# Projection, scores, output and routing of a gated layer in one step list, with two pairs of the shared expert moved behind the expert loop

## The chip, the cores and the metric

The program runs on one NeuronCore of a Trainium2 chip. TensorE (PE), VectorE (DVE), ScalarE (ACT), GpSimd (POOL) and SyncE (SP, which only issues transfers here) each work through their own list of instructions in order and wait on semaphores. The metric is the device time of one execution in microseconds; the kernel before has a median of 432.96 us over three runs (429.26 to 433.13).

## The reference

x is 32 x 64 tokens of 256 numbers, ctx the same; all float32. Four sublayers follow each other (layernorm before each):

```
# 1 gated retention, weights shared by q, k, v
Q,K,V = xh@Wh, kh@Wh, vh@Wh                       # two heads of 128; k = v = ctx
A  = max(|sum over batch of (Q K^T / sqrt(128)) * D|, 1)   # one 64x64 matrix per head
Y  = groupnorm(A V) ;  x += tanh(g) * ((relu(x@wg) * Y) @ wo)
# 2 mixture of 32 experts, 4 per token, at most 128 tokens each, and a shared expert
scores = sigmoid(x@gate.T); best 4 groups of 8, best 4 experts in them; slot = running count
routed = sum over 4 of w * (relu2(x_e @ up[e].T) @ down[e].T)
shared = relu2(x @ shup.T) @ shdn.T ;  x += tanh(g) * (routed + shared)
# 3 masked softmax(x ctx^T / 16) ctx ;  4 ternary-weight gated MLP (256 -> 1024 -> 256), int8 activations
```

A sums over all 32 sequences, so no output of sublayer 1 can start before every score is made. The slot of a token is its place in the order of all tokens, so no token can be gathered before the last one is routed.

## The kernel before, in words

The 2048 tokens are 16 tiles of 128, worked on in 8 pairs (NP = 8). Each engine has a block of code, and in it `run_steps(eng, n, stages)` writes out steps 0, 1, 2, ...: in step t each stage (lag, function) of the list is issued for pair t - lag, in the order of the list. So lags and places in the lists set the order on each engine, and `hold` puts the waits. Stages: c.sync waits for DVE's own instruction before.

Stage one, the scores loop: DVE p1_stats and p1_norm (POOL takes the power -1/2 in between, L469 and L471), PE p1_t transposes, ACT copies, PE p1_p multiplies by the gram matrix, DVE copies (p1_pt), PE p1_s adds to the scores, and p1_v makes the values from a ring of two ctxT buffers that ACT loads. DVE then turns the scores into A (L1052 to L1065).

Stage two, output and routing. PE per pair: p2_o (output product, psum<-big,bda), p2_zt (transposes, L798), p2_w (gate product, psum<-big,wg), p2_y (psum<-wo,tr), p2_xt (transposes, L816), p2_lg (logits, psum<-gateT,xnT), p2_pos (positions, five small products), p2_su and p2_sd (shared expert up and down, psum<-xnT,shup and psum<-shdn,rh), p2_ix (slots, psum<-gram,ck). DVE makes the statistics (o_stats, x1), the gate (wy), the routing in 17 parts (route_a) and 4 (route_b), adds the shared expert (`shared`, L1091) and the slots (add_slots). ACT normalises, copies and squares; POOL makes the rstd and the routing weights.

```
run_steps(pe, NP, [
    (1, p2_w), (3, p2_sd), (2, p2_xt), (0, p2_o), (2, p2_lg), (3, p2_pos), (2, p2_su), (1, p2_y),
    (3, p2_ix), (0, p2_zt)])
```

Stage three, experts: 16 steps of two experts. ACT writes the token indices, POOL gathers the tokens (L513), PE multiplies, DVE copies, SP stores; DVE also makes the ternary weights beside it. POOL writes the mask rows before it (L499, L502). Stage four: POOL gathers the expert rows (L531), DVE combines them (L1247), and attention and the MLP follow in one list of stages; DVE enters it when the norm weights (c_lnw) are in.

SP's transfers in order: constants, x in pairs, 11 weights and tables (c_w2, after half of the values), the expert weights upT and dnT, ctx and ctxT whole (after all values), xn stores, the three MLP matrices, expert output stores, the norm weights.

## Time and profile before

| | |
|---|---|
| median of three runs | 432.96 us (429.26 to 433.13) |
| profiled execution | 435.07 us, span of its instructions 432.6 us |
| busy in the span | PE 305.3 (71%), DVE 301.9 (70%), ACT 212.5 (49%), POOL 185.9 (43%) |
| mean granted clock of PE | 0.862 |
| moved | 43.89 MB, mean 101 GB/s |

The chain that ended last is 37% PE, 27% DVE, 12% issue, 11% DMA and 8% POOL. Busy shares are means over four stages with different limits, so the rows below are cut by stage: scores loop to 46.3 us, output and routing to 184.2 us, experts to 243 us, combine, attention and MLP to the end. A row of the windows view has, behind the stretch and its length, the busy time and the number of instructions of each engine, the granted clock of PE, the busy share of the DMA engines and GB/s.

### The profile page before, as it was taken

To read this page: it belongs to the slowest core of one execution; us is meant where nothing else is said; L and a number is where in the kernel's file an instruction comes from. 1 tells how busy PE (TensorE), PEld (TensorE's weight loads), DVE (VectorE), ACT (ScalarE), POOL (GpSimd) and SP (SyncE) were. 2 spreads that over 40 slices of the span, in tenths; PEclk is the share of its full clock that TensorE was granted. 3 is DMA by queue.
4 is the path that set the end of the run, shared out by engine and by line. 5 is a ranking of instruction groups with operands and counts; after the bars stand their busy time and mean duration, and the time that the engine had idled before them with its cause. 6 is when DMAs were issued, how large, how long until landed. Compare 5 with 4: busy or idle time off the path is not lost.

```text
span 432.6 us, 6083 instructions
## 1 busy us (share of the span) xinstructions
PE 305.3 (71%) x1780; PEld 231.1 (53%) x1780; DVE 301.9 (70%) x940; ACT 212.5 (49%) x384; POOL 185.9 (43%) x310
## 2 busy tenths in 40 slices
PE   2998489999999997348879403558664776667755
PEld 1886367888888776236768202325333344344423
DVE  2463335779787887717668334677999999989981
ACT  1232135334433535313333001557678989799883
POOL 3220121322233211576554177777878777332010
PEclk9998889999999998859899855555869899889898
DMA  5444799300000160035575532222121221100011
GB/s 179 121 139 145 291 436 371 116 27 6 19 25 26 33 284 24 1 79 145 129 160 171 153 103 79 80 73 74 50 74 55 68 85 36 51 26 0 26 46 52
DMA packets 23056, 43.89 MB, mean 101 GB/s; under 512 B 3630, under 2 KB 18416, under 8 KB 22128
## 3 DMA queue, kind: packets, MB, share of 16 engines
q1 hardware_dynamic: 16176, 28.82, 18.7%
q0 software_dynamic: 4672, 12.59, 11.3%
q10 hardware_dynamic: 2176, 2.10, 1.5%
q8 instruction: 14, 0.23, 0.2%
q14 instruction: 18, 0.15, 0.1%
HBM read 35.11 MB, written 8.39 MB: 101 GB/s over the span
## 4 chain that ended last, share of the span: by engine, by line
PE 37%; DVE 27%; issue 12%; DMA 11%; POOL 8%; ACT 5%; SPq 0%; POOLq 0%; DVEq 0%; ACTq 0%
PE psum L726 32%; DMA xn<-xn_dram,tix 6%; POOL big L531 5%; DVE x_all L1247 4%; DVE ham L1314 3%; DVE dnT L1312 3%; DVE upT L1304 2%; ACT rh L558 2%; DMA rh<-in_ctxT_dram 2%; DMA big<-ye_dram,dst_all 1%; DVE x_all L1272 1%; DVE bnx L1018 1%; PE psum L877 1%; DVE bn L1250 1%; DVE x_all L1336 1%
## 5 line engine op out<-in xcount | busy, mean ns | idle before, releaser
L531 POOL DMA_INDIRECT big<-ye_dram,dst_all x64 | 67.5, 1055 | 32.9 <-issue 18.9
L726 PE MATMUL psum<-q_w,rh 128*128 128x512 bf16 x128 | 40.9, 454 | 15.0 <-DVE upT L1304 9.1
L1247 DVE SCALAR_TENSOR_TENSOR x_all<-big,wk_all,x_all 128x256 f32<-128x256 f32 x64 | 31.1, 485 | 19.4 <-DMA big<-ye_dram,dst_all 17.6
L513 POOL DMA_INDIRECT xn<-xn_dram,tix x32 | 32.9, 1028 | 21.4 <-ACT tix L635 9.8
L726 PE MATMUL psum<-shdn,rh 128*128 128x256 f32 x128 | 31.4, 401 | 4.5 <-ACT rh L558 3.5
L917 PE MATMUL psum<-ident,xn 128*128 128x128 f32 x32 | 6.6, 341 | 34.2 <-ACT xn L592 34.2
L726 PEld LDWEIGHTS psum<-shdn,rh 128*128 128x128 f32 x128 | 24.8, 199 | 10.5 <-ACT rh L558 7.0
L726 PE MATMUL psum<-xnT,shup 128*128 128x256 f32 x128 | 29.6, 384 | 0.0
L726 PEld LDWEIGHTS psum<-q_w,rh 128*128 128x128 bf16 x128 | 12.5, 111 | 31.6 <-issue 20.5
L558 ACT ACTIVATE xnT<-psum 128x512 f32<-128x512 f32 x32 | 19.0, 595 | 18.6 <-PE psum L816 9.7
L457 POOL TENSOR_SCALAR vex<-mvx 128x2 f32<-128x2 f32 x16 | 3.6, 226 | 55.6 <-DVE mvx L1021 55.1
L457 POOL TENSOR_SCALAR ve<-mv 128x2 f32<-128x2 f32 x16 | 7.0, 438 | 46.2 <-DVE mv L1021 36.0
L726 PEld LDWEIGHTS psum<-xnT,shup 128*128 128x128 f32 x128 | 23.7, 190 | 2.9
L917 PEld LDWEIGHTS psum<-ident,xn 128*128 128x128 f32 x32 | 4.2, 169 | 37.3 <-issue 22.5
L558 ACT ACTIVATE big<-psum 128x512 f32<-128x512 f32 x16 | 9.6, 597 | 28.6 <-PE psum L752 20.9
L877 PE MATMUL psum<-ident,xn 128*128 128x128 f32 x64 | 14.3, 313 | 13.0 <-DMA xn<-xn_dram,tix 12.8
L558 ACT ACTIVATE dnT<-psum,q_down 128x512 bf16<-128x512 f32 x32 | 21.8, 682 | 3.4 <-PE psum L726 3.4
L592 ACT ACTIVATE xn<-x_all,sh,rs 128x256 f32<-128x256 f32 x16 | 8.7, 594 | 28.4 <-POOL sh L462 28.4
L690 ACT ACTIVATE upT<-upT 128x1024 f32<-128x1024 f32 x16 | 16.9, 1058 | 10.8 <-DVE upT L1304 10.8
L592 ACT ACTIVATE zr<-psum,sh,rs 128x256 f32<-128x256 f32 x16 | 8.2, 560 | 28.5 <-POOL sh L462 28.5
L635 ACT ACTIVATE tix<-idxf 128x1 int32<-128x1 f32 x32 | 6.1, 198 | 32.2 <-PE psum L877 25.5
L1304 DVE SCALAR_TENSOR_TENSOR upT<-psum,cgu,upT 128x1024 f32<-128x1024 f32 x16 | 20.5, 1278 | 1.7 <-PE psum L726 1.7
(191 smaller groups left out, 892.5 us busy)
## 6 DMA issues: line engine op xcount, KB each, us to landing
upT<-in_upT_dram SPq DMA_DIRECT2D x1, 4096.0 KB, 12.1
dnT<-in_dnT_dram SPq DMA_DIRECT2D x1, 4096.0 KB, 21.5
ye_dram<-rh SPq DMA_DIRECT2D x16, 256.0 KB, 2.7
rh<-in_ctxT_dram ACTq DMA_DIRECT2D x8, 256.0 KB, 3.1
x_all<-in_x_dram SPq DMA_DIRECT2D x8, 256.0 KB, 2.8
ctx_all<-in_ctx_dram SPq DMA_DIRECT2D x1, 2048.0 KB, 28.3
ctxT_all<-in_ctxT_dram SPq DMA_DIRECT2D x1, 2048.0 KB, 32.8
xn_dram<-xn SPq DMA_DIRECT2D x8, 256.0 KB, 2.1
```

The source lines that it names most:

```text
L513: pl.indirect_dma_start(out=xe[:, s, e, :], out_offset=None, in_=xn_dram[:, :], in_offset=bass.IndirectOffsetOnAxis(ap=tix[:, s, e:e + 1], ...
L531: pl.indirect_dma_start(out=gath[:, s, t * TOPK + k, :], out_offset=None, in_=ye_dram[:, :], in_offset=bass.IndirectOffsetOnAxis(ap=dst_al ...
L558: return act.activation(dst_ap, src, func, **kw).then_inc(done, 1)
L592: act.activation(dest[:, s, t, :], src(t), ACT.Identity, scale=rsb[:, s, t:t + 1], bias=sh[:, s, t:t + 1]).then_inc(done, 1)
L690: act.activation(sqj, hh[:, s, t, :], ACT.Square, accum_out=sst[:, s, t:t + 1]).then_inc(ssd[t], 1)
L726: return pe.matmul(o, l, r, start=first, stop=last, skip_group_check=True)
L877: ins = pe.transpose(bank(2, K, 2 * P)[:, k, e * P:(e + 1) * P], xe[:, s, e, k * P:(k + 1) * P], ident[:, :])
L917: ins = pe.transpose(bank(4, K, 2 * P)[:, k, t * P:(t + 1) * P], xn[:, s, t, k * P:(k + 1) * P], ident[:, :])
L1247: c(dve.scalar_tensor_tensor(xt(i, t), gath[:, s, t * TOPK + k, :], w, xt(i, t), ALU.mult, ALU.add))
L1304: dve.scalar_tensor_tensor(hh[:, s, t, :].rearrange("p (b n) -> p b n", b=2), psum[:, 2:4, :], cgu[:, s, 1, t:t + 1], sg[:, t, :].rearrang ...
L1312: dve.tensor_tensor(hw[:, s, t, :], hh[:, s, t, :], lnw[:, :], ALU.mult).then_inc(hwd[t], 1)
L1314: dve.tensor_reduce(ham[:, s, t:t + 1], hw[:, s, t, :], AX.X, ALU.max, apply_absolute_value=True)\
```

## The change

The two stages become one list of steps per engine. PE's list holds the scores loop (lags 0, 1, 2), the values (lag 8, so behind the scores), the transposes of A (10) and the output and routing pieces (12 to 20). The shared expert is cut into quarters (up and down, two halves each) at lags 17 to 20, and is run for the first six pairs only (NSH = 6); pairs 6 and 7 follow behind the expert loop, added by DVE in steps 1 and 2 of the combine loop. ctxT is loaded once by ACT, in eight transfers at the start, and kept; ctx comes in two parts, since its space holds the transposed xn of all pairs (xnT8) until the shared expert has used it. DVE's token rows (te) go to ACT (token_rows), POOL's mask work too. Logits move to the bank of positions, slots and values.

```diff
-            run_steps(pe, NP, [(0, p1_t), (1, p1_v), (1, p1_s), (0, p1_p)])
...
             run_steps(pe, NP, [
-                (1, p2_w), (3, p2_sd), (2, p2_xt), (0, p2_o), (2, p2_lg), (3, p2_pos), (2, p2_su), (1, p2_y),
-                (3, p2_ix), (0, p2_zt)])
+                (15, p2_lg), (20, early(p2_sd(0))), (13, p2_w), (17, p2_ix), (13, p2_zt), (12, p2_o), (0, p1_t),
+                (8, p1_v), (18, early(p2_su(1))), (16, p2_pos), (10, p1_at), (17, early(p2_su(0))), (1, p1_p),
+                (14, p2_xt), (19, early(p2_sd(1))), (2, p1_s), (13, p2_y)])
...
+            pe.wait_ge(xeT3, NG)
+            pe.wait_ge(hr3, NG)
+            for n in range(NSH, NP):
+                for h in range(2):
+                    p2_su(h)(Item(n), n % 2)
+            for n in range(NSH, NP):
+                for tt in (1, 0):
+                    p2_sd(tt)(Item(n), n % 2)
```

The waits that matter for the shared bank, and SP's list:

```diff
             def p2_lg(i, s):
-                hold(pe, (xnT2, i.at(1, 1)), *free(lt2, i))
+                hold(pe, (xnT2, i.at(1, 1)), (vc1, min(i.c + 7, NP)), (rb, RB * (i.c - 2) + 1))
...
             def p2_pos(i, s):
-                hold(pe, (ra, i.at(RA, RA_MASK)), *free(rb, i, RB), *free(ia2, i))
+                hold(pe, (ra, i.at(RA, RA_MASK)), (rb, RB * (i.c - 1) + 4), (lt2, min(i.c + 2, NP)), (ia2, i.c))
...
+            load_x(Item(0))
+            sp.dma_start(ident[:, :], a["c_ident"]).then_inc(c_in, 16)
+            sp.dma_start(whT[:, :, :], a["whT"]).then_inc(c_in, 16)
+            load_x(Item(1))
...
+            sp.wait_ge(lg2, NP)
+            for h in range(2):
+                sp.wait_ge(su2[h], NSH)
+            sp.dma_start(ctx_all[:, 0:2 * NSH, :], cv[:, 0:2 * NSH, :]).then_inc(c_ctx, 16)
...
+            for h in range(2):
+                sp.wait_ge(su2[h], NP)
+            sp.dma_start(ctx_all[:, 2 * NSH:NT, :], cv[:, 2 * NSH:NT, :]).then_inc(c_ctx2, 16)
             sp.wait_ge(yc3, NG)
             sp.dma_start(lnw, a["lnw"].to_broadcast([P, I])).then_inc(c_lnw, 16)
```

DVE's, ACT's and POOL's lists (the last two shown in part):

```diff
-            run_steps(dve, NP, [(0, p1_stats), (0, p1_norm), (1, p1_pt)])
...
+                (44, route_b(2)), (43, route_a(13)), (44, route_b(3)), (43, route_a(14)), (44, route_b(4)),
+                (43, route_a(15)), (43, route_a(16)), (2, p1_norm), (41, x1(0)), (42, route_a(0)), (41, x1(1)),
+                (42, route_a(1)), (41, x1(2)), (44, add_slots), (29, a_blocks), (42, route_a(2)), (42, route_a(3)),
+                (42, route_a(4)), (42, route_a(5)), (47, early(shared)), (42, route_a(6)), (42, route_a(7)),
+                (42, route_a(8)), (42, route_a(9)), (42, route_a(10)), (42, route_a(11)), (42, route_a(12)),
+                (40, wy), (4, p1_pt), (26, a_matrix), (43, route_b(0)), (43, route_b(1)), (39, o_stats),
+                (0, p1_stats)])
...
+            run_steps(act, NP, [
+                (13, affine), (19, early(square_shared)), (14, xn_), (16, token_rows), (14, copy_xnT), (8, p1_v),
+                (14, tanh_logits), (18, early(relu_shared(1))), (0, p1_t), (12, z), (17, early(relu_shared(0))),
+                (17, weight_abs)])
...
-            pl.wait_ge(su2, NP)
-            pl.wait_ge(mask_in, 16)
-            for b in range(2):
-                ins = pl.tensor_scalar(mnegb[:, :, b, :], msk8[:, :, :], -1.0, -NEG, ALU.add, ALU.mult)
...
+            for b in range(2):
+                act.activation(mnegb[:, :, b, :], msk8[:, :, :], ACT.Identity, scale=mscale[:, b:b + 1],
```

On PE, two pairs in the scores loop before (transposes of xn, values, scores, gram product):

```order
L752 MATMUL psum<-ident,xn 128x128 x4
L726 MATMUL psum<-wh,rh 128x128 x4
L726 MATMUL psum<-rh,tr 64x64 x8
L726 MATMUL psum<-big,gram 128x256 x2
L752 MATMUL psum<-ident,xn 128x128 x4
```

and now the end of that loop, up to the first output product (psum<-big,bda):

```order
L775 MATMUL psum<-ident,xn 128x128 x4
L751 MATMUL psum<-big,gram 128x256 x2
L751 MATMUL psum<-ctxT_all,tr 64x64 x8
L751 MATMUL psum<-wh,ctxT_all 128x128 x4
L751 MATMUL psum<-big,gram 128x256 x2
L751 MATMUL psum<-ctxT_all,tr 64x64 x8
L751 MATMUL psum<-wh,ctxT_all 128x128 x4
L751 MATMUL psum<-ctxT_all,tr 64x64 x8
L751 MATMUL psum<-wh,ctxT_all 128x128 x4
L797 MATMUL psum<-ident,tr 128x64 x2
L751 MATMUL psum<-wh,ctxT_all 128x128 x4
L751 MATMUL psum<-big,bda 128x2x128 x2
```

The values (psum<-wh) have left the pairs of the loop; two stand before the last scores, two around the transposes of A, and four behind the first output product. A full step of output and routing on PE before:

```order
L726 MATMUL psum<-big,bda 128x2x128 x2
L726 MATMUL psum<-gateT,xnT 128x32 x4
L726 MATMUL psum<-mm,tri 128x32
L726 MATMUL psum<-mcum,ones 128x32
L726 MATMUL psum<-mm,tri 128x32
L726 MATMUL psum<-mm,ones 128x32
L726 MATMUL psum<-mcum,ones 128x32
L726 MATMUL psum<-xnT,shup 128x256 x8
L726 MATMUL psum<-wo,tr 128x256 x4
L726 MATMUL psum<-gram,ck 128x32 x8
L798 MATMUL psum<-ident,zr 128x128 x4
L726 MATMUL psum<-big,wg 128x256 x4
```

and now part of one, from the logits on (positions left out in the middle of the order):

```order
L751 MATMUL psum<-gateT,ctx_all 128x32 x4
L751 MATMUL psum<-big,wg 128x256 x4
L751 MATMUL psum<-gram,ck 128x32 x8
L820 MATMUL psum<-ident,zr 128x128 x4
L751 MATMUL psum<-big,bda 128x2x128 x2
L751 MATMUL psum<-ctx_all,shup 128x256 x4
...
L751 MATMUL psum<-ctx_all,shup 128x256 x4
L836 MATMUL psum<-ident,xn 128x128 x4
L751 MATMUL psum<-shdn,rh 128x256 x4
L751 MATMUL psum<-wo,tr 128x256 x4
L751 MATMUL psum<-gateT,ctx_all 128x32 x4
```

The shared products come in groups of four between the others instead of eight in a row. On PE at the end of the expert loop, now:

```order
L915 MATMUL psum<-ident,zr 128x128 x2
L751 MATMUL psum<-dnT,tr 128x256 x2
L751 MATMUL psum<-ctx_all,shup 128x256 x16
L751 MATMUL psum<-shdn,upT 128x256 x16
L947 MATMUL psum<-ident,xn 128x128 x4
```

Where the transposes of the combine loop (L917 before) followed the last expert's product at once, two pairs of the shared expert lie between them.

## Rows read from the trace of the kernel before

**Rows 1.** Windows by stage, and one full step; columns as told above
```profile
49.00:66.50 17.50, 11.41 (x45) 8.74 (x46) 5.20 (x15) 5.18 (x11) 3.83 (x12) 0.80 0.97 420
66.50:170.50 104.00, 97.98 (x575) 83.17 (x573) 82.98 (x415) 41.75 (x71) 26.79 (x80) 1.00 0.25 92
94.17:108.22 14.05, 13.72 (x82) 11.72 (x82) 11.71 (x59) 5.81 (x10) 4.03 (x12) 1.00 0.06 19
170.50:184.20 13.70, 6.32 (x31) 5.12 (x31) 10.61 (x40) 6.24 (x11) 5.64 (x8) 0.76 0.00 1
184.20:243.00 58.80, 46.14 (x288) 38.26 (x288) 37.44 (x80) 19.14 (x60) 32.87 (x32) 0.88 0.55 138
246.90:300.00 53.10, 21.86 (x69) 13.35 (x70) 28.51 (x77) 19.38 (x40) 40.89 (x53) 0.50 0.28 85
```

**Rows 2.** Timeline, scores loop, PE and DVE: start, length, engine, line, operation
```profile
21.62 0.73 DVE L1036 TENSOR_SCALAR xn<-x_all,mv,rs 128x256 f32<-128x256 f32 x2 [1.13 <-POOL rs L471]
22.31 0.69 DVE L1047 COPY tr<-psum 128x512 f32<-128x512 f32 x1
22.41 0.66 PE L752 MATMUL psum<-ident,xn 128*128 128x128 f32 x4
...
22.91 1.06 PE L726 MATMUL psum<-wh,rh 128*128 128x128 f32 x8
22.92 0.74 DVE L1018 BATCH_NORM_STATS2 bn<-x_all 128x6 f32<-128x256 f32 x2
...
23.58 0.38 DVE L1021 BATCH_NORM_AGGREGATE mv<-bn 128x2 f32<-128x6 f32 x2
...
23.89 1.15 PE L726 MATMUL psum<-rh,tr 128*64 128x64 f32 x16
...
24.97 1.13 PE L726 MATMUL psum<-big,gram 128*128 128x256 f32 x4
...
37.06 1.53 PE L726 MATMUL psum<-rh,tr 128*64 128x64 f32 x16
...
38.52 2.08 PE L726 MATMUL psum<-big,gram 128*128 128x256 f32 x4
```

**Rows 3.** Timeline, from the last scores to the first transposes of z
```profile
46.34 0.28 DVE L1052 TENSOR_TENSOR tr<-psum,dn 64x128 f32<-64x128 f32 x1 [1.27 <-PE psum L726]
...
48.96 1.10 PE L726 MATMUL psum<-big,bda 128*128 128x256 f32 x4 [1.12 <-issue]
...
53.94 1.12 PE L798 MATMUL psum<-ident,zr 128*128 128x128 f32 x4 [3.88 <-ACT zr L592]
```

**Rows 4.** Groups by form in the full step 94.17 to 108.22: busy, mean
```profile
L726 PE MATMUL psum<-shdn,rh 128*128 128x256 f32 x16 | 3.7, 386 | 0.3 <-ACT rh L558 0.3
...
L726 PE MATMUL psum<-big,wg 128*128 128x256 f32 x8 | 1.9, 379 | 0.0
...
L1182 DVE TENSOR_TENSOR gram<-wh,tokid 128x256 f16<-128x256 f32 x1 | 0.4, 413 | 0.0
```

**Rows 5.** Timeline, last pair's logits to the first token gather
```profile
163.69 1.08 PE L726 MATMUL psum<-gateT,xnT 128*128 128x32 f32 x8 [0.69 <-ACT xnT L558]
...
170.64 5.41 PE L726 MATMUL psum<-shdn,rh 128*128 128x256 f32 x16 [1.52 <-ACT rh L558]
...
175.92 2.04 POOL L499 TENSOR_SCALAR shup<-msk 2x1024 bf16<-2x1024 uint8 x2
...
184.16 1.19 POOL L513 DMA_INDIRECT xn<-xn_dram,tix  x1 [3.89 <-ACT tix L635]
```

**Rows 6.** Timeline, from the experts into the combine loop
```profile
246.85 0.99 POOL L531 DMA_INDIRECT big<-ye_dram,dst_all  x1 [12.29 <-DMA ye_dram<-rh]
...
253.52 2.11 DVE L1247 SCALAR_TENSOR_TENSOR x_all<-big,wk_all,x_all 128x256 f32<-128x256 f32 x4 [9.91 <-DMA big<-ye_dram,dst_all]
...
265.01 1.08 PE L917 MATMUL psum<-ident,xn 128*128 128x128 f32 x4 [22.12 <-ACT xn L592]
```

**Rows 7.** Transfers by line: count, KB each, us from issue to landing
```profile
upT<-in_lnw_dram SPq DMA_DIRECT2D x1, 512.0 KB, 4.7
```

More of the change, by code:

```diff
@@ L37 @@
 HS = 512
+NSH = 6
 NHS = HS // P
@@ new lines, in relu_shared, with stage @@
+            def relu_shared(h):
+                def stage(i, s):
+                    hold(act, (su2[h], i.c + 1), (sd2, i.c - 1 if i.c < NSH else 0))
+                    dest = rh if i.c < NSH else rh_late
+                    copy_to(dest[:, s, h * 512:(h + 1) * 512], bank(6 + h), rl2[h], ACT.Relu)
+                return stage
+            def square_shared(i, s):
+                hold(act, (rl2[0], i.c + 1), (rl2[1], i.c + 1))
+                dest = rh if i.c < NSH else rh_late
+                copy_to(dest[:, s, :], dest[:, s, :], sq2, ACT.Square)
@@ new lines, in token_rows, with weight_abs @@
+            def token_rows(i, s):
+                hold(act, (ra, i.at(RA, RA_MASK)), (ix2, i.c))
+                for tt in range(2):
+                    act.activation(te[:, tt, :], oh[:, tt, :, :].rearrange("p k e -> p (k e)"), ACT.Copy,
+                                   scale=tokid[:, 2 * i.c + tt:2 * i.c + tt + 1]).then_inc(tes, 1)
+            def weight_abs(i, s):
+                n = i.c - 5
+                if n < 0:
+                    return
+                hold(act, (c_w4, 48))
+                act.activation(q_w[:, n, :], wraw[:, n, :], ACT.Abs, accum_out=wabs[:, n:n + 1]).then_inc(wq_a, 1)
@@ L810, in p2_xt @@
             def p2_xt(i, s):
-                last = i.j is None and i.c == NP - 1
-                hold(pe, (xn2, i.at(2, 2)), (aff, i.at(1, 1 if last else 2)))
+                hold(pe, (xn2, i.at(2, 2)), (aff, min(i.c + 2, NP)))
                 for t in range(2):
@@ L841, in p2_sd, with stage @@
+            def p2_sd(t):
+                def stage(i, s):
+                    src = rh if i.c < NSH else rh_late
+                    hold(pe, (sq2, i.c + 1), (sa2, i.c if i.c < NSH else NSH))
                     for n in range(NHS):
-                        ins = mm_(bank(4, 2, D)[:, t, :],
-                                  rh[:, s, n * 256 + t * P:n * 256 + (t + 1) * P],
+                        ins = mm_(bank(5 if i.c < NSH else i.c - 4, 2, D)[:, t, :],
+                                  src[:, s, n * 256 + t * P:n * 256 + (t + 1) * P],
@@ L957, in stage @@
                 def stage(i, s):
-                    hold(pe, (qT5, i.c + 1), *[(b[0], min(i.c + b[1], NP)) for b in before])
+                    hold(pe, (qT5, i.c + 1), (sa2, NP if w else 0), *[(b[0], min(i.c + b[1], NP)) for b in before])
                     for b in range(2):
@@ L1078, in wy, with x1, stage @@
                                          ALU.max, ALU.mult).then_inc(wy2, 1)
[L1080 to L1087 removed]
+            def x1(part):
+                def stage(i, s):
+                    c = Chain(x2, i, 5, (0, 1, 3)[part])
+                    if part == 0:
+                        hold(dve, (y2, i.at(1, 1)))
+                        c(dve.scalar_tensor_tensor(x_all[:, tiles(i), :], bank(4, 2, D), tg[:, 0:1],
+                                                   x_all[:, tiles(i), :], ALU.mult, ALU.add))
+                        return
+                    for tt in range(2):
+                        if part == 1:
+                            if tt == 0:
+                                c.sync()
+                            c(dve.bn_stats(bnx[:, s, tt, :], xt(i, tt)))
+                        else:
+                            if tt == 0:
+                                c.sync()
+                            c(dve.bn_aggr(mvx[:, s, tt, :], bnx[:, s, tt, :]))
+                return stage
             def shared(i, s):
                 hold(dve, (sd2, i.at(1, 1)))
[L1091 to L1092 removed]
+                dve.scalar_tensor_tensor(x_all[:, tiles(i), :], bank(5 if i.c < NSH else i.c - 4, 2, D), tg[:, 2:3],
+                                         x_all[:, tiles(i), :], ALU.mult, ALU.add).then_inc(sa2, 1)
             def route_a(part):
```

262 lines of the change are left out of this document (122 added, 140 removed).

## Prediction

> **What bounds the kernel now.** I read the windows by stage first [rows 1]. They show a stretch from 66.5 to 170.5 us in which PE is busy 97.98 of 104 us at full clock, and around it stretches in which nobody is: 11.41 of 17.5 us before it (clock 0.80), 6.32 of 13.7 us behind it (0.76). One full step inside it, 14.05 us for one pair of tiles, has PE at 13.72 and DVE at 11.71. Then I read the timeline of the loop that makes the scores [rows 2], of the passage from the scores to the output product [rows 3], the groups of one full step [rows 4], and the timelines of the last pair's routing [rows 5] and of the passage from the experts to the combine loop [rows 6]. Up to 184.16 us, where the first token gather leaves, the kernel is bound by PE's list where it is full and by latencies at both ends; the 58.8 us of experts behind it run at PE 46.14; from 246.85 POOL's gathers feed the combine loop (POOL 40.89 of 53.1 us).
>
> **Step 1, the scores loop.** One pair costs PE 0.66 + 1.06 (values) + 1.15 + 1.13 us, period 3.8; DVE's four pieces are 0.69, 0.73, 0.74 and 0.38, or 2.54 [rows 2]. The change takes the 1.06 out and starts the normalising two steps late, so that POOL's round trip is covered. Left are PE 2.9 less overlap and DVE 2.54: I take 2.7 per pair. The first transpose comes at about 9.0 us (0.8 sooner than the old one, since x is first in SP's queue and two constants are enough to start). Eight pairs give 9.0 + 21.6 = 30.6; the last scores stand two steps behind with two values in between, 33.0. From the end of the scores to the first output product it took 48.96 - 46.34 = 2.6 [rows 3]: that product starts at 35.6 instead of 48.96, **13.4 us sooner**. If PE gains nothing from the missing values the period is 3.8 and all this is 4.5 us; if only DVE counts, 2.54, 14.6 us.
>
> **Step 2, filling.** I number PE's new steps from the first output product. The five first hold work of some 3.6 pairs without the shared expert (14.05 less the two shared groups of 3.7, with their overlap 7.1, is 6.95 a pair [rows 1, 4], 25.0 us), four values (4.1) and the latency from output product to transposed z, 53.94 - 48.96 = 5.0 [rows 3], which output product, value and gate product (1.9 [rows 4]) cover but for 1.3; as much again is open before the first product of the gated z. Together 31.5.
>
> **Step 3, full steps.** Each piece of one pair lies in another step now, so a step costs the dearer of PE and DVE. DVE: 11.71 less the token rows (0.41, now two activations on ACT) and the shared addition where it is missing: 11.2. PE: 6.95 and the quarters of the shared expert (1.8 each), which come in one by one: 8.8, 10.6, 12.5, then 13.1 without the output product, then 9.2 without its other pieces (DVE 10.0 there). The dearer ones: 11.2 + 11.2 + 12.5 + 13.1 + 10.0 = 58.0. The last pair's logits start at 35.6 + 31.5 + 58.0 = 125.1; before, 163.69 [rows 5].
>
> **Step 4, the tail.** From those logits to the first gather it took 184.16 - 163.69 = 20.5 us, with the shared group at 5.41 instead of 3.7 (clock 0.76 [rows 1]). POOL's mask work, 2.04 for its first two operations there [rows 5], lies beside DVE and is on nobody's path; it becomes two activations behind the experts, where ACT waits, and counts nothing. But the new order puts two pairs' worth of quarters between logits and slots: the last logits (1.1), eight quarters of 1.8 and 1.6 of small products, 17.1 on PE before the last slots, and 1.8 from there to the gather: 18.9. Gather without losses: 144.0.
>
> **Step 5, what two full queues lose.** Before, DVE had 17% to spare beside PE; now both are over 85% full in eight steps, with in-order lists that wait on each other at ten places a step. The trace has no such stretch. Bounds: nothing, as PE's 0.33 open of 14.05 shows that a list can be full, and 17% of those 110 us, 19 us, which is DVE's idle share in the full step [rows 1]. I take 8%, nearer to the full list, because by the new orders most producers stand a whole step ahead: **9 us, gather at 153**, 31.2 sooner.
>
> **Step 6, experts.** 62.7 us from first gather to first row gather [rows 5, 6], unchanged. Their weights (8 MB) are asked for once the context is in, long before the old 45 us; 1.5 MB of context are loaded while the last routing runs and could meet the first gathers: +0 to +3, taken as 0, since the sums of the ternary weights are ready sooner.
>
> **Step 7, two shared pairs behind the experts.** PE, idle from 243 to 265.01 [rows 6], gets four groups of 3.7: 14.8 us at full clock, ending at 258. ACT and DVE are idle there too (late additions 0.74 each, in steps where DVE waits for gathers). One thing is late: SP loads 0.5 MB of context and the norm weights only when the shared up products are done, at 243 + 7.4 = 250.4. The weights took 4.7 us to land [rows 7]; with the context ahead, about 257, and DVE's first combine started at 253.52 [rows 6] and waits for them. But the next steps wait for POOL's sixteen gathers: 3.5 us late there cost 0.5. If the clock is not full the groups take up to 29.6 us (the shared group of 5.41 was measured over a change of clock; doubled is the upper bound), until 272.6, and hold the transpose of 265.01 by 7.6. I take full clock: the full stretch up to 170.5 is at 1.00, the experts at 0.88 with their slow start in it [rows 1], and the four groups follow them almost without a wait. By the Trainium skill (TensorE: Matmul & The Clock Gate, "Part 1: The HAM clock gate") an idle array is throttled and sustained work releases it; that speaks for 14.8 us here.
>
> **Sum.** Gather 153 + 62.7 + the rest of the old span from 246.85 (185.8) + 0.5 = 402.0 us span, against 432.6. The profiled execution was 435.07, 2.5 above its span: 404.5. The median of the runs before is 432.96, 2.1 below the profiled one: **402 us**.
>
> **Rivals.**
> *DVE sets the steps* (0.17). For: 11.71 of 14.05. If its idle 17% stay, a step is 11.2/0.83 = 13.5: five steps 67.5 instead of 58.0, the one before +4, the tail's DVE part +3: about 17 in all instead of my 9. Time 410.
> *The half clock comes into the scores loop* (0.08). With the values gone PE's list is thinner there. Against: 2.9 of 2.7 us is not thin. At half clock the scores and gram products take 1.53 and 2.08, as at 37.06 and 38.52 us [rows 2], a step some 1.5 longer: eight steps, 12 us: 414. The Trainium skill says of the same page and part that the gate follows how busy the array was, so this rule speaks against taking work out of that loop; the sum by it would be 414 instead of 402. The first steps behind the scores, 0.80 before [rows 1], are where it is likelier to show, at 3 us.
> *The late shared pairs are not hidden* (0.10): half clock, transposes held by 7.6 and the combine's start by another 3: 413.
> *Better than taken* (0.14): no loss in step 5, and the experts start at full clock: 392.
> *The two lists lock* (0.04), the one on the slow side. Logits, positions, slots and values share one bank now: the logits of pair k wait for DVE's first slot operation of pair k-2, which is near the end of DVE's step, behind the addition that waits for PE's last product of a step. If that product is the one of the step just before, PE waits in every step for half of DVE's 11.2, 5.6 us: in eight steps +45, 447 us. By the orders a whole PE step lies between them; it decides from six such steps on (34 us) whether the kernel is slower than before.
> Forecast 0.47.
>
> **Range and chances.** What a measurement can tell from no change is 1%, 4.3 us. From 392 (best case) to 418 (late pairs, clock or DVE together with 3 us of traffic) leaves out the lock and sums of two mishaps, about 2 in 10 with the far end of the good case. Faster by over 1%: all but the lock and a mixture of mishaps, 0.94; within 1% 0.02; slower 0.04.
>
> **What the new profile would show.** Step 1: first output product at 34 to 38 us, period 2.6 to 2.9. Step 3: in the full steps PE 92% or more where four quarters lie, DVE over 90% in the two before. Steps 4 and 5: first token gather at 147 to 160. Step 7: PE at 1.00 up to 258, norm weights landing near 257, first transpose of the combine loop 80 to 82 us after the first token gather (80.9 before). Wrong would be: an output product after 42, a step over 15 us, positions or logits that wait for DVE by more than 2 us in each step, or a gap of more than 84 us from token gather to that transpose.

## The result

| | median of runs | lowest to highest | profiled execution | its span |
|---|---|---|---|---|
| before | 432.44 us (4 runs) | 429.26 to 433.13 | 435.07 us | 432.6 us |
| changed | 400.01 us (4 runs) | 398.69 to 401.18 | 400.74 us | 398.9 us |

The ratio is 0.9281, 95% interval 0.9231 to 0.9331. The forecast of 402 is 2.0 us above the median; by spans it is 402.0 against 398.9. That closeness is partly luck: two terms were 5.4 us and some 9 us off in opposite directions.

### The profile page after: what moved, and what is told of

The parts are those of the page before. It is cut to its first block, busy times and chain, and to the rows that moved or that the text cites. A ratio compares the mean times of both kernels' runs of the same rounds, so it can differ in the third digit from the quotient of the medians.

```text
span 398.9 us, 6186 instructions
## 1 busy us (share of the span) xinstructions
PE 299.1 (75%) x1772; PEld 227.0 (57%) x1780; DVE 295.2 (74%) x932; ACT 219.9 (55%) x410; POOL 184.9 (46%) x310
## 4 chain that ended last, share of the span: by engine, by line
DVE 33%; PE 27%; issue 14%; DMA 11%; POOL 9%; ACT 4%; SPq 1%; POOLq 0%; DVEq 0%; ACTq 0%
PE psum L751 24%; DMA xn<-xn_dram,tix 7%; POOL big L540 6%; DVE x_all L1292 4%; DVE ham L1363 3%; DVE dnT L1361 3%; DVE upT L1353 3%; DMA x_all<-in_x_dram 2%; DVE x_all L1321 1%; DVE bnx L1048 1%; PE psum L898 1%; DVE bn L1048 1%; PE psum L775 1%; DVE x_all L1385 1%; DVE ck L1229 1%
## 5 line engine op out<-in xcount | busy, mean ns | idle before, releaser
L751 PEld LDWEIGHTS psum<-q_w,rh 128*128 128x128 bf16 x128 | 12.2, 109 | 32.4 <-issue 20.5
L751 PE MATMUL psum<-ctx_all,shup 128*128 128x256 f32 x128 | 30.3, 385 | 0.0
L751 PEld LDWEIGHTS psum<-ctx_all,shup 128*128 128x128 f32 x128 | 23.5, 190 | 2.8
L567 ACT ACTIVATE big<-psum 128x512 f32<-128x512 f32 x16 | 9.5, 597 | 26.8 <-PE psum L775 17.1
L751 PE MATMUL psum<-shdn,rh 128*128 128x256 f32 x96 | 22.6, 384 | 1.5 <-DVE x_all L1133 1.0
L751 PE MATMUL psum<-q_w,dnT 128*128 128x256 bf16 x128 | 21.3, 322 | 0.8 <-ACT dnT L567 0.8
L898 PE MATMUL psum<-ident,xn 128*128 128x128 f32 x64 | 14.2, 306 | 9.4 <-DMA xn<-xn_dram,tix 9.1
L751 PE MATMUL psum<-ident,dnT 128*128 128x128 f16 x128 | 14.2, 240 | 9.3 <-ACT dnT L567 7.0
L1363 DVE TENSOR_REDUCE ham<-dnT 128x1 f32<-128x1024 f32 x16 | 19.5, 1220 | 0.6
L567 ACT ACTIVATE dnT<-dnT,q_up,hs 128x1024 f32<-128x1024 f32 x16 | 19.7, 1233 | 0.2 <-DVE hs L1379 0.2
L751 PEld LDWEIGHTS psum<-shdn,rh 128*128 128x128 f32 x96 | 17.6, 190 | 3.8 <-issue 1.1
L1361 DVE TENSOR_TENSOR dnT<-upT 128x1024 f32<-128x1024 f32 x16 | 19.5, 1217 | 0.3
L567 ACT ACTIVATE xnT<-psum 128x512 f32<-128x512 f32 x24 | 14.3, 596 | 9.6 <-PE psum L898 6.7
```

Source lines behind the costliest of these rows:

```text
L567: return act.activation(dst_ap, src, func, **kw).then_inc(done, 1)
L751: return pe.matmul(o, l, r, start=first, stop=last, skip_group_check=True)
L898: ins = pe.transpose(bank(2, K, 2 * P)[:, k, e * P:(e + 1) * P], xe[:, s, e, k * P:(k + 1) * P], ident[:, :])
L1361: dve.tensor_tensor(hw[:, s, t, :], hh[:, s, t, :], lnw[:, :], ALU.mult).then_inc(hwd[t], 1)
L1363: dve.tensor_reduce(ham[:, s, t:t + 1], hw[:, s, t, :], AX.X, ALU.max, apply_absolute_value=True)\
```

## The profile after

The first part of the page (busy time, share of the span, number of instructions):

```profile
PE 299.1 (75%) x1772; PEld 227.0 (57%) x1780; DVE 295.2 (74%) x932; ACT 219.9 (55%) x410; POOL 184.9 (46%) x310
```

PE is busy 6.2 us less than before, DVE 6.7 less: most of the 33.7 us saved was idle time. The windows answer to [rows 1]; columns are as there (stretch, its length, busy time of PE, its weight loads, DVE, ACT, POOL with counts, the granted clock, DMA share, GB/s). The first ends at the first output product, the second at the logits of the third pair, the next five lie between the logits of successive pairs, then the tail, the experts, and the passage to the first transposes of the combine loop:

```profile
11.90:41.04 29.14, 27.00 (x227) 22.28 (x227) 17.56 (x54) 6.57 (x11) 6.84 (x13) 1.00 1.05 409
41.04:75.45 34.41, 30.05 (x167) 25.38 (x166) 22.97 (x106) 16.70 (x34) 11.94 (x36) 0.95 0.07 27
75.45:84.89 9.44, 8.78 (x59) 7.38 (x58) 8.99 (x49) 4.43 (x10) 2.89 (x9) 0.99 0.08 30
84.89:95.85 10.96, 10.43 (x67) 8.78 (x65) 10.51 (x59) 5.03 (x11) 4.24 (x12) 1.00 0.07 24
95.85:107.81 11.96, 11.89 (x74) 10.27 (x73) 11.51 (x65) 6.46 (x13) 5.12 (x15) 1.00 0.07 24
107.81:120.39 12.58, 12.58 (x78) 11.11 (x77) 11.47 (x58) 6.35 (x13) 3.33 (x10) 1.00 0.28 92
120.39:129.13 8.74, 8.74 (x58) 7.68 (x57) 8.25 (x48) 4.53 (x9) 2.74 (x8) 1.00 0.71 291
129.13:149.71 20.58, 18.27 (x116) 15.51 (x115) 15.42 (x80) 12.92 (x23) 2.82 (x8) 1.00 0.25 78
149.71:210.15 60.44, 50.44 (x318) 42.25 (x317) 40.07 (x85) 20.07 (x62) 33.46 (x32) 0.94 0.57 140
210.15:228.67 18.52, 10.03 (x48) 8.52 (x46) 6.67 (x15) 6.95 (x9) 14.42 (x17) 0.83 0.46 142
```

What is to be seen: in the five full steps the busier of PE and DVE is idle for 0 to 0.45 us of a step; by busy time DVE leads in the first two, PE from the third on. The front is where idle time is left: 11.90 us before the first transpose, 4.4 us of PE in the fill, 2.3 in the tail.

The timeline of the start (start, length, engine, line, operation, in brackets the idle time before and its releaser):

```profile
0.80 5.80 ACTq L572 DMA_DIRECT2D ctxT_all<-in_ctxT_dram  x8
...
7.93 0.21 ACT L575 ACTIVATE tg<-gates 128x4 f32<-128x4 f32 x1
...
8.23 0.75 DVE L1048 BATCH_NORM_STATS2 bn<-x_all 128x6 f32<-128x256 f32 x2 [8.23 <-ACT tg L575]
...
10.16 0.75 DVE L1048 BATCH_NORM_STATS2 bn<-x_all 128x6 f32<-128x256 f32 x2 [0.88 <-DMA x_all<-in_x_dram]
...
11.90 1.12 PE L775 MATMUL psum<-ident,xn 128*128 128x128 f32 x4 [1.83 <-DVE xn L1065]
```

ScalarE issues the eight context loads for 5.80 us and only then loads its table and makes the tanh; DVE waits for that tanh (L1238 stands ahead of its whole list), and then for x of the second pair, whose loads are under way beside the context's: x takes 9.4 us to land in the median here, 2.8 before (the page's list of transfers). Two things differ between these numbers. Before, at most two loads of x and two of the context were open at a time; here SyncE also issues its eight loads of x and then the eleven weights and tables without a wait.

One period of the scores loop and the passage behind it, which answer to [rows 2, 3]:

```profile
20.31 0.66 PE L775 MATMUL psum<-ident,xn 128*128 128x128 f32 x4
20.80 1.03 PE L751 MATMUL psum<-big,gram 128*128 128x256 f32 x4
21.76 1.15 PE L751 MATMUL psum<-ctxT_all,tr 128*64 128x64 f32 x16
22.84 0.66 PE L775 MATMUL psum<-ident,xn 128*128 128x128 f32 x4
```
```profile
37.06 1.15 PE L751 MATMUL psum<-ctxT_all,tr 128*64 128x64 f32 x16
...
38.24 0.28 DVE L1082 TENSOR_TENSOR tr<-psum,dn 64x128 f32<-64x128 f32 x1 [2.55 <-PE psum L751]
...
41.04 1.03 PE L751 MATMUL psum<-big,bda 128*128 128x256 f32 x4
```

The period is 22.84 - 20.31 = 2.53 us, the three PE groups end to start. The last pair's transposes start at 30.42, its scores at 37.06, the output product at 41.04.

The tail, which answers to [rows 5]:

```profile
146.65 1.90 ACT L641 ACTIVATE q_w<-big 128x2048 bf16<-128x2048 f32 x1
...
146.85 0.19 DVE L1236 TENSOR_TENSOR idxf<-psum,idxf 128x32 f32<-128x32 f32 x1 [1.48 <-PE psum L751]
...
148.54 0.48 ACT L653 ACTIVATE tix<-idxf 128x1 int32<-128x1 f32 x4
...
149.71 1.19 POOL L522 DMA_INDIRECT xn<-xn_dram,tix  x1 [7.37 <-ACT tix L653]
...
151.38 0.28 PE L751 MATMUL psum<-wabs,onesf 128*128 128x3 f32 x2
...
153.65 1.07 PE L898 MATMUL psum<-ident,xn 128*128 128x128 f32 x4 [1.99 <-DMA xn<-xn_dram,tix]
```

The token index is complete at 147.04, but ScalarE is in a pass over the ternary weights (L641) until 148.5. PE is done with the sixth pair's shared products at 151.5 and waits 1.99 us for the gathered tokens before it starts on the experts (L898). The passage behind the experts, which answers to [rows 6]:

```profile
206.20 7.07 PE L751 MATMUL psum<-ctx_all,shup 128*128 128x256 f32 x32
213.11 7.07 PE L751 MATMUL psum<-shdn,upT 128*128 128x256 f32 x32
...
219.43 2.05 DVE L1292 SCALAR_TENSOR_TENSOR x_all<-big,wk_all,x_all 128x256 f32<-128x256 f32 x4 [12.34 <-DMA big<-ye_dram,dst_all]
...
228.67 1.09 PE L947 MATMUL psum<-ident,xn 128*128 128x128 f32 x4 [8.49 <-ACT xn L592]
```

Both late groups run at full clock (32 products in 7.07 us, as 16 in 3.72 in a full step) and end 8.5 us before PE is needed again. The norm weights are asked for at 213.77 and take 5.2 us, against 4.7 in [rows 7]; the first combine starts half a microsecond behind them, 9.28 behind the first row gather against 6.67 before. The transposes come 18.52 us behind the row gather against 18.16 before.

Where the 33.7 us of span came from: the first token gather is 34.45 us sooner (149.71 for 184.16), the experts 2.25 us shorter (60.44 for 62.69), what follows the first row gather 3.0 us longer (188.75 for 185.75).

## The experiments

Each was timed beside the kernel before, in three later series, with ratios to it; the changed kernel's is 0.9281. Before had medians of 433.35, 434.11 and 433.35 us there, against 432.44 in the first series, and the changed kernel was not timed again: a difference of medians from its 400.01 us holds 1 to 2 us of doubt. Where ratios below have wide intervals, as with no late pair, the kernel before spread from 425.84 to 441.75 us beside them. "Gather" is the first token gather.

**Late shared pairs: none and one.**

```diff
-NSH = 6
+NSH = 8   # every shared pair ahead of the experts; the second context load is left out
```


> The shared expert of pairs 6 and 7 goes back into the step list, nothing behind the experts. My account (those 14.1 us of PE work are free behind the experts and not free in front): one quarter of 1.8 us more before the last slots, and some 9 of the other 12.4 us stand between the last slots and the first expert transposes, which now wait 7.2 us for gathers: total 10 to 12 us above the changed kernel, 411, and the combine loop starts 0.5 us sooner. Rival (the late pairs cost as much behind as they save in front, the gain came from the one list alone): 398 to 402.

```diff
-NSH = 6
+NSH = 7
```


> Only pair 7 stays behind the experts. If each late pair saves its own work: half of the way between the changed kernel and the run with none late, 405 to 406. If the first transposes' wait of 7.2 us for gathers hides one pair (3.6 us of it are in use): 402 to 403.

Measured: 415.09 us for none (411.38 to 415.60; ratio 0.9656, 0.946 to 0.9851), 407.11 for one (405.83 to 408.91; 0.9379, 0.9322 to 0.9435), 400.01 for two. Each pair that moves behind the experts is worth 8.0 and 7.1 us, together 15.1 where 10 to 12 were expected; PE's work on two pairs is 14.1 us. The other 17.3 of the 32.4 us between the medians belong to the one list with all that came with it; of these runs only the next one takes a part out of it, the place of the values. The timeline of the tail with none late shows how the late pairs gain:

```profile
149.39 0.19 DVE L1235 TENSOR_TENSOR idxf<-psum,idxf 128x32 f32<-128x32 f32 x1 [2.56 <-PE psum L750]
...
160.57 1.06 ACT L566 ACTIVATE rh<-rh 128x1024 f32<-128x1024 f32 x1
...
161.53 0.47 ACT L652 ACTIVATE tix<-idxf 128x1 int32<-128x1 f32 x4
...
162.68 1.19 POOL L521 DMA_INDIRECT xn<-xn_dram,tix  x1 [18.88 <-ACT tix L652]
...
164.70 3.69 PE L750 MATMUL psum<-shdn,rh 128*128 128x256 f32 x16 [0.94 <-DVE x_all L1132]
...
168.23 0.28 PE L750 MATMUL psum<-wabs,onesf 128*128 128x3 f32 x2
168.37 0.63 PE L897 MATMUL psum<-ident,xn 128*128 128x128 f32 x4
```

The index is complete at 149.6, 2.5 us later than with two late pairs, but the copy that releases the gather is last in ScalarE's list, behind the squares of the last shared products, and starts 11.9 us later. The gathers stand at 162.68 (none late), 156.45 and 149.71. It is tempting to blame that copy, but PE does not wait for it: PE is on the shared products from the last slots at 149.00 on (busy 16.58 of 19.37 us) and makes the first expert transposes right behind them, at 168.37, with the tokens already there. From the last logits to those transposes it takes 37.78 us with none late, 30.78 with one and 24.52 with two: 7.0 and 6.3 us a pair, where PE's products of a pair take 7.07. So the late pairs gain through PE's list, as expected. Only with two late does PE wait for the gathered tokens (1.99 us). No run moves the copy alone, so what a sooner one would give is not shown. Of the remaining difference, 1.4 us lies in two steps of output and routing (20.99 us for 19.57, see the start below), which other kernels show with two late pairs as well. With none late the transposes follow the row gather by 18.19 us, with two by 18.52: the two late pairs cost 0.3 behind the experts.

**The values back in the scores loop** (all the rest as changed).

```diff
-                (8, p1_v), ...   # PE, and the same on ACT
+                (1, p1_v), ...
```


> The values go back into the scores loop (lag 1 on PE and ACT), the rest as changed. My account: the loop's period goes from 2.53 to about 3.5 us, 7.7 us more, the four values between last scores and output product are gone, 4.3 less, so the output product comes 3.4 us later; behind it four values less, of which latencies keep about half, 2 us sooner: total +1 to +3 us. Rival (values in the loop are what cost the kernel before its 8 us): +6 to +9. Rival (PE's thin loop matters more than its work): -1 to -3.

Measured: 406.04 us (404.12 to 408.57; 0.9492, 0.9322 to 0.9661), 6.0 above: +1 to +3 were expected, and the first rival, values in the loop as a main cost of the kernel before, fits instead. The period of the loop is 3.42 us for 2.53. The output product starts at 46.70, 5.66 later, and the logits of the second pair at 71.10, 24.4 us behind it; with the values behind the scores that is 24.28. The windows of output product to second logits, this kernel's and the changed one's:

```profile
46.70:71.10 24.40, 19.89 (x93) 15.79 (x94) 13.33 (x56) 9.50 (x19) 7.30 (x23) 0.93 0.06 22
```
```profile
41.04:65.32 24.28, 21.81 (x127) 18.64 (x126) 13.32 (x56) 12.27 (x24) 7.30 (x23) 1.00 0.07 27
```

Without the four values PE has idle time where they stood, and a lower clock. The fill is a chain of latencies with room for them, so there they are free; in the loop a pair's values cost 0.89 us of their 1.06.

**More work on DVE in each step; the output product twice.** Both add useless work, the result is unchanged.

```diff
+                            dve.tensor_tensor(spare[:, :, :], o3, o3, ALU.add)   # twice per pair, 128x384
```


> DVE does two useless additions of 128x384 (about 0.45 us each, 0.9 to 1.0 with their wait) in each pair's step, ahead of the first routing part. Step account (a step costs the dearer of PE and DVE): only the three or four steps before the shared expert is complete, and the tail, lengthen, +3 to +5 us in all. Rival (DVE sets all steps): +7 to +8. Rival (PE sets all): 0 to +1.

```diff
-                for h in range(H):
+                for h in (0, 1, 0, 1):
```


> PE makes each output product twice (0.87 us more in each of eight steps). Step account: hidden in the steps that DVE sets, full in the three with most shared work, and in the first ones it covers waits: +3 to +4 us. Rival (PE sets all steps): +7. Rival (DVE sets all): 0 to +1.

Measured: DVE 404.62 us (403.67 to 407.75; 0.9463, 0.9284 to 0.9642), 4.6 above the changed kernel and as expected; PE 401.80 (401.50 to 403.37; 0.9385, 0.923 to 0.9541), 1.8 above, half of what was expected and within the doubt between series. Each addition on DVE takes 0.56 us, 1.11 per pair; a second output product takes PE 0.86. The windows with more DVE work, between successive logits:

```profile
78.08:88.42 10.34, 8.95 (x59) 7.24 (x58) 9.86 (x51) 4.43 (x10) 3.19 (x9) 1.00 0.08 27
88.42:100.41 11.99, 10.80 (x66) 8.62 (x65) 11.51 (x61) 5.02 (x11) 4.64 (x12) 1.00 0.07 23
100.41:113.22 12.81, 12.28 (x75) 10.12 (x74) 12.33 (x66) 6.45 (x13) 5.33 (x15) 1.00 0.06 22
113.22:125.80 12.58, 12.58 (x78) 11.11 (x77) 12.13 (x59) 6.34 (x13) 3.95 (x10) 1.00 0.27 96
125.80:135.19 9.39, 8.95 (x58) 7.55 (x57) 8.94 (x47) 4.53 (x9) 3.15 (x8) 1.00 0.65 264
```

The steps grow by 0.90, 1.03, 0.85, 0 and 0.65. The rule (a step costs the dearer of PE and DVE) gives this: DVE's busy time in the changed kernel plus 1.11 is 10.10, 11.62, 12.62, 12.58 and 9.36, against PE's 8.78, 10.43, 11.89, 12.58 and 8.74; the dearer one is within 0.4 us of the measured 10.34, 11.99, 12.81, 12.58 and 9.39. With the product twice the first two steps, and the one with most work that has an output product, read:

```profile
66.78:75.35 8.57, 7.55 (x47) 6.46 (x45) 8.09 (x44) 4.43 (x10) 3.27 (x10) 1.00 0.09 32
75.35:86.35 11.00, 9.78 (x62) 7.87 (x61) 10.55 (x59) 4.54 (x10) 4.25 (x12) 1.00 0.08 26
...
97.44:110.13 12.69, 12.69 (x78) 11.03 (x77) 12.24 (x66) 6.35 (x13) 5.70 (x16) 1.00 0.06 23
```

The first two take 19.57 us, as the same two do in the changed kernel (65.32 to 84.89), though PE has more to do; there its clock was 0.84 in the first, here 1.00. It is 1.00 with the product once, too, in the kernel with the sooner weight pass below, and the two steps take 19.58 us. So in this stretch, which DVE sets, neither that drop of the clock nor more PE work showed in the sum. The step led by PE grows from 11.96 to 12.69, nearly the whole 0.86. I expected three such steps; the other two hold no output product, which is why the total grew by less. The rest of the added time stands in the fill (25.65 us for 24.28).

**The start: the tanh, and who issues the context loads.** Three kernels, each with the wait for the tanh where DVE first uses it. The second also issues the loads behind the tanh on ScalarE, the third has SyncE issue them instead, one behind each later load of x.

```diff
-            dve.wait_ge(tg_ok, 1)
...
-                        hold(dve, (y2, i.at(1, 1)))
+                        hold(dve, (y2, i.at(1, 1)), (tg_ok, 1))
```


> DVE waits for the tanh of the gates only where it first uses it, not at its head. In the changed kernel ACT issues eight ctxT loads (5.80 us) before it, and DVE's first statistics start at 8.23 right behind it. If the tanh is what starts it late: statistics at 6.7 or before, total 1 to 1.5 us less. If x's landing is what counts (second pair at 10.16, waited for by DVE): 0 to 0.4 less.

> As the run before, and ACT issues the eight ctxT loads behind the tanh, so that x and the first constants do not share the DMA engines with them at the start. If the contention of these loads is the rest of the late start (first transposes at 11.90, 9.84 in the kernel before): first transposes at 9.0 to 9.8, total 2 to 3 us less than the changed kernel. If only the issue order mattered: as the run before.

```diff
-                act.dma_start(ctxT_all[:, :, tok(i)], ctv[:, :, tok(i)]).then_inc(c_ct[n], 16)
...
+            for n in range(2, NP + 2):
+                if n < NP:
+                    load_x(Item(n))
+                i = Item(n - 2)
+                sp.dma_start(ctxT_all[:, :, tok(i)], ctv[:, :, tok(i)]).then_inc(c_ct[n - 2], 16)
```


> The start of the changed kernel is 5.4 us later than forecast, and by theory this is the queue of ScalarE: eight context loads (5.80 us of issues) stand ahead of the tanh, and they share the DMA engines with the first loads of x. Here the context loads are issued by SyncE, each behind a later load of x, and DVE waits for the tanh only where it first uses it. Theory: first transposes near 8.1 us instead of 11.9, period unchanged at 2.5, first output product near 37.2 instead of 41.0, first token gather near 146 and the total 3 to 4 us lower, 396 to 397. Rival one (the landing of the quarters of x sets the loop, whoever issues the context loads): output product at 39 or later, total 398 to 400. Rival two (the values behind the scores wait for the context loads that are now late): scores sooner, but the first gate logits not, total 399 to 401.

| | first transposes | output product | gather | median | ratio to before |
|---|---|---|---|---|---|
| changed | 11.90 | 41.04 | 149.71 | 400.01 | 0.9281 (0.9231 to 0.9331) |
| tanh's wait later | 11.80 | 41.27 | 151.38 | 400.42 | 0.9219 (0.9178 to 0.926) |
| and loads behind the tanh | 8.11 | 39.33 | 148.02 | 399.51 | 0.9206 (0.9161 to 0.9251) |
| loads by SyncE | 8.86 | 37.85 | 147.95 | 396.70 | 0.9134 (0.9088 to 0.918) |

The wait alone gave nothing (1 to 1.5 us were expected if the tanh counted, 0 to 0.4 if x did): DVE's first statistics start at 4.47, but those of the second pair wait for x until 10.05, as in the changed kernel (10.16). With the loads later on ScalarE x lands in 5.4 us, and another wait takes over, on the timeline:

```profile
5.34 5.56 ACTq L574 DMA_DIRECT2D ctxT_all<-in_ctxT_dram  x8
...
10.96 0.38 ACT L576 ACTIVATE gram<-psum 128x256 f32<-128x256 f32 x1 [5.41 <-issue]
...
12.85 1.91 PE L750 MATMUL psum<-big,gram 128*128 128x256 f32 x4
```

ScalarE copies the gram product behind its eight issues, and the loop's first product with it (psum<-big,gram) starts only at 12.85. With SyncE issuing, the output product comes 3.2 us sooner, theory 3.8. Only 1.8 of it is left at the gather, in the profiled execution. The windows show where the other 1.4 went, two steps which together take 20.99 us for 19.57:

```profile
62.12:71.63 9.51, 7.60 (x43) 6.30 (x41) 9.03 (x50) 4.43 (x10) 4.08 (x13) 0.90 0.08 28
71.63:83.11 11.48, 10.96 (x58) 9.23 (x57) 9.73 (x52) 4.31 (x10) 3.40 (x10) 0.78 0.07 25
```

PE is at 0.78 of its clock in the second, where it was at 0.99, and busy 10.96 us with 58 products where 59 took 8.78. Here the low clock fell on a step in which it leads. This is not shown to come from the new start: in the profiled executions the same two steps take 20.99 to 21.00 us, at 0.90 and then 0.78 or 0.79, also with the tanh's wait later, with no late pair and with all edits together, and 19.55 to 19.59 in all other kernels without added work. How often each case comes is not known. The median is 3.3 us lower, 396.70, and all six runs (394.47 to 398.73) lie below the lowest of the sooner weight pass, timed beside it (399.29): the total gain of this start is shown. Where the 1.5 us beyond the gather's 1.8 arise is not: with the loads behind the tanh the gather is as early (148.02) and the median 399.51.

**Norm weights ahead of the late context** on SyncE.

```diff
+            sp.wait_ge(yc3, NG)
+            sp.dma_start(lnw, a["lnw"].to_broadcast([P, I])).then_inc(c_lnw, 16)
             for h in range(2):
                 sp.wait_ge(su2[h], NP)
             sp.dma_start(ctx_all[:, 2 * NSH:NT, :], cv[:, 2 * NSH:NT, :]).then_inc(c_ctx2, 16)
```


> SP loads the norm weights before it waits for the late shared products and loads the last part of ctx. My account: DVE's first combine starts 6.7 us after the first row gather instead of 9.3, but the loop behind is paced by POOL's gathers, so the total changes by 0 to -0.6 us. Rival (the late weights cost their whole 2.6 us): -2.6.

Measured: 400.83 us (399.74 to 402.94; 0.9242, 0.9197 to 0.9286). The first combine comes 7.35 us behind the row gather instead of 9.28, the transposes 18.33 instead of 18.52. The total did not fall (0 to 0.6 less was expected): the combine's own start was covered by the gathers, as the 0.5 us of step 7 had it.

**The token index: the third weight pass one stage sooner; three late pairs; all together.**

```diff
-                (17, weight_abs)])
+                (16, weight_abs)])
```


> In the tail of the changed kernel the copy that releases the token gather comes 1.7 us behind the last index product, behind the third pass of the absolute values of the ternary weights (1.90 us on ScalarE). Here that pass stands one stage sooner in ScalarE's list. Theory: first token gather at 148.2 instead of 149.7, total 1 to 1.7 us lower, 398.3 to 399. Rival: the weights land too late for the sooner place, ScalarE stands there, and gather and total are unchanged or up to 2 us later.

```diff
-NSH = 6
+NSH = 5
...
-                if 1 <= i.c < 1 + NP - NSH:
-                    shared(Item(NSH + i.c - 1), s)
+                for n in {1: (5, 6), 2: (7,)}.get(i.c, ()):
+                    shared(Item(n), s)
```


> Three late pairs instead of two (pairs 5, 6 and 7; the norm weights are asked for ahead of the late context, and all three late additions lie in the first two waits of the combine loop). Theory: the tail is then bound by DVE and by its chain rather than by TensorE, so of the 7.1 us of a pair's shared products 3 to 4 are saved in front (gather near 146); behind the experts TensorE ends near 227.4 - 3.5, just ahead of the first transposes of the combine loop, 78.96 after the gather: total 396 to 397. Rival one (TensorE alone sets the tail, as the steps from seven to six pairs suggest): the full 7 us, total 393. Rival two (the late products now hold the combine loop): the transposes 80 or more after the gather, total 399 to 402.

> The three edits together: context loads from SyncE behind x, the third pass of absolute values sooner, and three late pairs. They act at three places one after another (start, last routing, tail), so by theory the gains add: 3.5 + 1.5 + 3.5 below the changed kernel, 391 to 393 us. Rival: the tail can give its time only once, and the sum is at the best single edit, 395 to 397.

| | last logits to index | to gather | transposes behind gather | median | ratio to before |
|---|---|---|---|---|---|
| changed | 17.72 | 20.58 | 78.96 | 400.01 | 0.9281 (0.9231 to 0.9331) |
| weight pass sooner | 17.72 | 19.12 | 80.52 | 400.59 | 0.9238 (0.9198 to 0.9279) |
| three late pairs | 17.98 | 19.38 | 81.84 | 401.43 | 0.9238 (0.92 to 0.9276) |
| all three edits | 16.67 | 18.07 | 82.19 | 395.51 | 0.9125 (0.9075 to 0.9175) |

The sooner pass takes 1.46 us out of the tail, as expected; its start was 0.8 later and its experts 1.6 longer in the profiled execution, and no gain shows in the median (1 to 1.7 us were expected). PE could use only part of it: from the last logits to the first expert transposes it takes 23.46 us for 24.52. The timeline of its tail:

```profile
144.60 1.90 ACT L641 ACTIVATE q_w<-big 128x2048 bf16<-128x2048 f32 x1
...
147.64 0.19 DVE L1236 TENSOR_TENSOR idxf<-psum,idxf 128x32 f32<-128x32 f32 x1 [1.48 <-PE psum L751]
...
147.86 0.48 ACT L653 ACTIVATE tix<-idxf 128x1 int32<-128x1 f32 x4 [0.33 <-DVE idxf L1236]
```

The kernels with three late pairs also ask for the norm weights ahead of the late context, and hold some products of PE and copies of ScalarE longer, for the buffers that the third pair shares. Three late pairs alone gained nothing (the theory's 3 to 4 us fell). The windows of the last stretch before the index, alone and with the other edits:

```profile
141.15:147.75 6.60, 5.88 (x31) 4.83 (x31) 3.56 (x19) 4.48 (x6) 1.40 (x4) 0.74 0.01 4
```
```profile
138.21:143.12 4.91, 4.20 (x31) 3.65 (x31) 3.58 (x18) 2.31 (x4) 1.20 (x4) 1.00 0.02 5
```

The same 31 products take 5.88 us at clock 0.74 and 4.20 at 1.00, with PE ahead of DVE's last operation both times. The profiled execution of the three late pairs took 405.64 us, 4.2 above its own median, so its row above and its clock are that execution's; whether the clock fell in the others too is not known. The rest of this paragraph goes by the kernel with all three edits. Even at full clock the third pair gave 1.05 us up to the index, 16.67 for 17.72, of its 7.1: by DVE's 14.58 us there, the chain of the last pair's routing, and no longer PE's work, sets that time. PE then waits 5.34 us for the gathered tokens, so its list is no longer what holds the experts. Behind the experts the third pair took 7.1 more of PE's idle time (1.86 us left of 8.99 before the transposes), and the transposes came 82.19 us behind the gather for 80.52 with the weight pass alone. All edits together: 395.51 us (393.87 to 401.03), where 391 to 393 were expected and the rival had 395 to 397; 4.5 below the changed kernel and the best median here. But 396.70 of the start alone is within its interval, so only the start's gain is shown.

## Why the prediction was right, step by step

**Step 1 (output product at 35.6)** was 5.4 us too early: 41.04. The period was 2.53, not 2.7, worth -1.4 over eight pairs. The start was +2.9: "x is first in SP's queue" overlooked that ScalarE issues eight loads into the same DMA engines, and the tanh behind them. The three start kernels show this as the cause: with the context loads moved the first transposes come at 8.11 and 8.86, with only the tanh's wait moved at 11.80. The Trainium skill says it (DMA: Bandwidth & Descriptors, "Issuing engines are not separate DMA queues": loads from different engines interleave on the same DMA engines); the trace agrees, as x takes 9.4 us to land with the context loads beside it and 5.4 with them 4.5 us later, and I had not looked it up. Not all of 9.4 for 2.8 before is theirs: even interleaved in one queue it is 6.2, and no run has the old limit of two open loads. The drain was +2.5: eight periods end at 32.1, and the last scores start 4.9 behind that, where I had charged 2.4. Behind the last transposes PE still has two gram products, two groups of scores and two values, and it is busy 8.48 of the 8.92 us from 32.12 to the output product. From the start of the last scores to the output product it is 3.98 for the 2.6 I took from their end: +1.4, of which 1.15 is the group of scores itself. The rival "half clock in the scores loop" fell: 1.00, PE 27.00 of 29.14 us. Its price was also read too low: the scores group of 1.53 us at 37.06 ran at a mean clock of 0.68, not at half; only the gram product of 2.08 did (0.50).

**Step 2 (31.5; its terms add up to 31.7)** took 34.4. PE's work was 30.05 against 29.1 forecast; idle time of PE 4.4 against 2.6. The kernel with the values in the loop shows that the four values, which I charged at 4.1, were free here; so beside the 25.0 us of other work the latencies were worth 9.4 us, and not 2.6. The clock fell where I had said it was likelier, at 0.84 for the step from 65.32 to 75.45 us, but DVE led that step (9.65 of 10.13) and the doubled product shows it cost nothing.

**Step 3 (58.0)** took 53.7: 9.44, 10.96, 11.96, 12.58, 8.74 for 11.2, 11.2, 12.5, 13.1, 10.0. The terms of PE (8.8, 10.6, 12.5, 13.1, 9.2) were right within 0.6; DVE's 11.2 in the first two was too much, it had 8.99 and 10.51 to do. Part of this was the sum: 11.71 less 0.41 for the token rows is 11.3, and less the 0.74 of the shared addition, which those steps lack, 10.6. That is the second step; the first has less still, since the old step's whole work is not there before the last lags set in. The rule, the dearer of PE and DVE, held; the added work confirmed it.

**Step 4 (18.9)** took 20.6. Up to the last slots it was right, 17.33 us for 17.1; 1.5 us is ScalarE's weight pass ahead of the token index, which I did not see in the order. Moving it took 1.46 out of the way to the gather.

**Step 5 (9 us for two full queues)** was wrong. The dearer engine's busy times in the five steps sum to 8.99 + 10.51 + 11.89 + 12.58 + 8.74 = 52.71 us of 53.68: 2% lost, not 8%. The term stood for all 110 us of filling, full steps and tail; these three took 34.41 + 53.68 + 20.58 = 108.7 us, and without the term I had 108.4 for them. So it measured about 0.3 in the sum, where I had taken 9. That the total was close comes from this term covering +5.4 (step 1), +2.9 (step 2) and +1.7 (step 4): with -4.3 (step 3) and -9 they make -3.3, gather at 149.7 for 153. The rival "DVE sets the steps" was half right, on who leads at first, and wrong on the price; "the two lists lock" fell, no step is over 12.58 us.

**Step 6 (62.7)** took 60.4, with the clock at 0.94 instead of 0.88. The other variants, with the same expert loop, took 60.7 to 64.4, so I claim no cause.

**Step 7 (0.5)** held: 18.52 for 18.16 us, against 18.19 with no late pair. Norm weights landed 8.9 us behind the row gather (forecast 10.2), PE ended 10.0 behind it at full clock (11.2). By the Trainium skill (TensorE: Matmul & The Clock Gate, "Part 1: The HAM clock gate") sustained work releases the throttle; the trace agrees, with 7.07 us for each 32 products. The gain in front is work taken out of PE's list there: from the last logits to the first expert transposes it takes 24.52 us with two late pairs, 30.78 with one and 37.78 with none.

From the first row gather to the end it was 188.75 us, not 186.3. Of this, 2.6 lies behind the first transposes of the combine loop (170.2 for 167.6). The other variants have 165.5 to 169.4 there (172.9 in the execution of the three late pairs that lay above its median), and the one without late pairs 168.4: before lies inside that spread, the changed kernel's profiled execution above it, so this is no cost of the change that a run shows.

## What to carry over

Where every producer stands a full step ahead of its user in all lists, price a step at the dearer engine's work and next to no loss (2% here), and put the doubt into filling, draining and the last item's chain instead: there each queue's order counts. A small copy that leaves late behind a long pass is not yet a loss: look first whether the engine that it releases in the end is free. Here one left 11.9 us late while PE still had work of its own, and making another leave 1.46 us sooner moved PE by 1.06. A load moved to another engine's queue still competes with the first loads that the pipeline waits for, and its issues delay what stands behind them: issue it behind those loads, from an engine with nothing to compute. Work moved into a later idle stretch is free only as long as its own stage stays bound by it: the first two pairs gave 15.1 us, the third about 1 ahead of the gather and none in the median.

## What the runs showed of the hardware

Eight loads of 256 KB issued by ScalarE occupied it for 5.45 to 5.80 us, 0.7 us each, with no computation between them. With them at the same time, as many loads of x on SyncE's queue took 9.4 us to land in the median; with them issued 4.5 us later, 5.4; with SyncE issuing both in turn, 6.2. Before, with at most two of each open at a time, it was 2.8.

Kernels that differ only elsewhere show TensorE's clock differently in the two steps behind the second pair's logits: 0.84 and 0.99 in the changed kernel, 1.00 and 1.00 with the sooner weight pass, 0.90 and 0.79 with the tanh's wait later. They take 19.57, 19.58 and 20.99 us: the low clock cost nothing where DVE led, and 1.4 us where PE did.
